# A two-layer graph network kernel: two of every 192 edge tiles fetched row by row from SyncE's queue

## What is computed

```python
h_s, h_v = s @ lin1_ws * a, v @ lin1_wv * a            # one row of 160 numbers for each node
w = silu(edge_scalars @ fc_w1) @ fc_w2                 # weights of each edge
es, ev = h_s[edge_src], h_v[edge_src]                  # gather: one row for each edge
m = ... w, es, ev, edge_attr ...                       # messages, 320 or 512 numbers an edge
agg = segment_sum(m, edge_dst)                         # add into the destination nodes
out = layernorm(x + node_update(agg, x))
```

## Time and profile before

| | us |
|---|---|
| median of 3 runs | 4140.89 |
| the runs | 4140.88, 4140.89, 4152.81 |
| the profiled execution | 4138.21 |
| span of its trace | 4136.5 |
| layer 0, first to last gather issued by POOL | 49.4 to 2003.3 |
| layer 1, first to last gather issued by POOL | 2099.9 to 4058.2 |

### The profile page before, as it was taken

How to read it: one execution, slowest core, us unless ns; L and a number is a source line. 1 busy time by engine, 2 the same in 40 slices (tenths; PEclk the granted TensorE clock), 3 DMA queues, 4 the chain that set the end, 5 groups by cost and what they waited for, 6 DMA issues and landing times. The chain is left out here.

```text
span 4136.5 us, 230757 instructions
## 1 busy us (share of the span) xinstructions
PE 3309.1 (80%) x91130; PEld 2547.6 (62%) x91131; DVE 2370.1 (57%) x6475; ACT 2897.3 (70%) x12105; POOL 3001.8 (73%) x3196
## 2 busy tenths in 40 slices
PE   8888888888777777777888888888878777777777
PEld 6666666666555555555766666666656565566556
DVE  6555555555444444444556666666666666666667
ACT  6666666666666666666477777777778777777776
POOL 5777777777777777777457777777777777777771
PEclk9999999999999999999999999999999999999998
DMA  5333333333222222222244334434333333333333
GB/s 156 83 84 84 83 83 83 83 86 83 73 73 73 72 73 73 73 73 72 83 123 108 104 105 109 106 104 108 105 105 98 94 94 96 94 94 96 94 94 111
DMA packets 361345, 381.19 MB, mean 92 GB/s; under 512 B 173457, under 2 KB 282677, under 8 KB 361182
## 3 DMA queue, kind: packets, MB, share of 16 engines
q0 software_dynamic: 150048, 256.28, 24.1%
q1 hardware_dynamic: 209936, 122.14, 10.4%
q10 hardware_dynamic: 1296, 1.91, 0.2%
HBM read 356.28 MB, written 23.76 MB: 92 GB/s over the span
## 5 line engine op out<-in xcount | busy, mean ns | idle before, releaser
L552 POOL DMA_INDIRECT e_rows<-scratch_table,k_index x3126 | 2954.9, 945 | 998.8 <-issue 886.1
L581 ACT ACTIVATE e_match<-e_match,e_attr 128x40 f32<-128x40 f32 x10976 | 2476.7, 316 | 0.0
L617 PE MATMUL e_sum<-e_match,e_msg 128*32 128x40 f32 (+1 forms) x81536 | 1440.6, 215 | 677.3 <-DVE e_msg L817 342.8
L617 PEld LDWEIGHTS e_sum<-e_match,e_msg 128*32 128x32 f32 x81536 | 1295.0, 111 | 995.8 <-DVE e_msg L820 376.4
L812 DVE TENSOR_TENSOR e_msg<-e_w,e_rows 128x512 f32<-128x512 f32 x784 | 541.9, 691 | 1656.4 <-DMA e_rows<-scratch_table,k_index 1608.5
L574 ACT ACTIVATE e_hidden<-e_h 100x512 f32<-100x512 f32 (+1 forms) x784 | 384.2, 490 | 1124.4 <-PE e_h L597 1116.6
L610 PE MATMUL e_w<-k_fc,e_hidden 100*128 100x192 f32 (+1 forms) x6272 | 1030.7, 367 | 0.8 <-issue 0.8
L610 PEld LDWEIGHTS e_w<-k_fc,e_hidden 100*128 100x128 f32 (+1 forms) x6272 | 812.3, 190 | 351.0 <-issue 333.0
L597 PE MATMUL e_h<-e_inputs,k_fc 128*100 128x512 f32 (+1 forms) x1568 | 713.3, 537 | 116.4 <-issue 63.7
L815 DVE TENSOR_TENSOR e_msg<-e_w,e_rows 128x384 f32<-128x384 f32 x784 | 428.7, 547 | 0.0
L817 DVE TENSOR_TENSOR e_msg<-e_w,e_rows 128x384 f32<-128x384 f32 x784 | 428.6, 547 | 0.0
(11 more groups left out here) (131 smaller groups left out, 1021.1 us busy)
## 6 DMA issues: line engine op xcount, KB each, us to landing
e_inputs<-in_inputs SPq DMA_DIRECT2D x196, 256.0 KB
e_rows<-scratch_table,k_index POOLq DMA_INDIRECT x3126
e_attr<-in_edge_attr SPq DMA_DIRECT2D x392, 24.0 KB
e_inputs<-in_inputs SPq DMA_DIRECT2D x196, 40.0 KB
e_xb<-in_xT SPq DMA_DIRECT2D x50, 128.0 KB
scratch_yT<-m_yT SPq DMA_DIRECT2D x10, 640.0 KB, 4.5
e_xb<-scratch_yT SPq DMA_DIRECT2D x50, 128.0 KB
k_index<-in_src SPq DMA_DIRECT2D x396, 4.0 KB, 3.2
```

The costliest lines, as they stand in the source:

```text
L552: pool.indirect_dma_start(out=rows[j][:, t, :], out_offset=None, in_=table_dram, in_offset=bass.IndirectOffsetOnAxis(ap=index[k][:, c:c + ...
L581: last = nc.scalar.activation(match[j][:, t, c, :], match[j][:, t, 4, :], ACT.Copy, scale=attr[q][:, e0 + t, e:e + 1])
L617: return nc.tensor.matmul(out[32 * g:32 * g + 32, c0:c0 + n, :], m[:, f:f + 32], m5[:, which:which + n, :], start=first and opens, stop=en ...
```

## The change

In each layer, after two bodies as before, the other 96 bodies run in 8 spans of 12. In bodies 5 and 11 of a span, counted from 0 (`FETCHED`), the last tile of group 1 is no longer gathered by POOL: POOL issues three gathers for that group (the last of them raises the semaphore by 32 in place of 16). That is 16 tiles a layer, 32 in all, so 3126 indirect DMAs become 3094.

These 32 tiles are fetched by SP. It reads their row numbers from a new small tensor, `row_index` (one 16x16 load for each span), eight numbers at a time into registers (`TENSOR_LOAD`), and issues one DMA for each row, 128 a tile, into `kept_rows[0]` or `kept_rows[1]`. A batch is one such load with its eight DMAs. `BATCHES` says how many batches stand behind the loads of q = 0 and q = 1 in each body of a span: (2, 1) in the first five bodies, 32 batches in twelve bodies in all. `attr[q]` is loaded in the middle of the first batch of its half. When a tile is complete, and group 1 of the body before is summed, SP issues one DMA that copies `kept_rows` to the fourth tile of `rows[1]` (`place_rows`).

A new semaphore, `placed`, goes up by 16 for each body: by the copy in the two bodies with a fetched tile, by an instruction of SP in the ten others, behind all their batches. DVE now also waits for it ahead of group 1's messages in every body, and SP waits for it once at the start of a span.

The loops become longer. In the built program POOL's branch goes back over 275 instructions (before 43), SP's over 841 and 793 (before 47 and 39). The loops of PE, DVE and ACT stay as they were; DVE's go back over 237 and 232 instructions, PE's over 317 and 314 in layer 0 and 436 in layer 1.

The core of the diff:

```diff
+FIRST, SPAN = 2, 12
+SPANS = (BODIES - FIRST) // SPAN
+BATCH = 8
+FETCHED, FETCHED_GROUP = (5, 11), 1
+BATCHES = ((2, 1),) * 5 + ((1, 1), (1, 1), (2, 1), (1, 1), (2, 1), (2, 1), (2, 0))
+PER_TILE = P // BATCH
...
+            def fetch_rows(batch, between=None):
+                which, batch = divmod(batch, PER_TILE)
+                _, numbers = nc.values_load_multi_w_load_instructions(
+                    row_index[batch:batch + 1, which * BATCH:which * BATCH + BATCH], engines=[sp.engine], min_val=0, max_val=NPAD - 1,
+                    skip_runtime_bounds_check_because="sources are node numbers")
+                for r in range(BATCH):
+                    if between and r == BATCH // 2:
+                        between()
+                    p = batch * BATCH + r
+                    sp.dma_start(kept_rows[which][p:p + 1, :], table_dram[bass.ds(numbers[r], 1), :]).then_inc(row_in[which], 16)
+
+            def place_rows(span, which):
+                landed, summed = 16 * P * (span + 1), GPB * (FIRST + SPAN * span + FETCHED[which] - 1) + FETCHED_GROUP + 1
...
+                sp.wait_ge(row_in[which], landed)
+                sp.wait_ge(sum_done, summed)
+                sp.dma_start(rows[FETCHED_GROUP][:, TPG - 1, :], kept_rows[which][:, :]).then_inc(placed, 16)
...
+            def fetching_body(span, position, with_base):
+                i, batch = FIRST + SPAN * span + position, sum(sum(b) for b in BATCHES[:position])
+                for q, batches in enumerate(BATCHES[position]):
+                    load_inputs(i, q, (2 * (position % 2) + q + 2) % INDEX_BUFFERS)
+                    if position == 0 and q == 0:
...
+                        sp.wait_ge(row_index_in, landed)
+                        sp.wait_ge(placed, free)
+                    if q == 1 and position in FETCHED:
+                        place_rows(span, FETCHED.index(position))
+                    for b in range(batches):
+                        fetch_rows(batch + b, (lambda: load_attr(i, q)) if b == 0 else None)
+                    batch += batches
+                    if not batches:
+                        load_attr(i, q)
+                if position not in FETCHED:
+                    sp.sem_inc(placed, 16)
+                if with_base:
+                    load_base(i)
+                if with_base and L == 1:
+                    store_self(i - 1)
+
+            def spans(first, last, with_base):
+                with sp.Fori(first, last) as span:
+                    for position in range(SPAN):
+                        fetching_body(span, position, with_base)
+                    load_row_index(span + 1)
...
+            spans(0, SPANS // 2, True)
             if L == 1:
                 store_self(NT - 1)
...
+            spans(SPANS // 2, SPANS, False)
...
+            def gather(i, position, j):
+                k = 2 * (position % 2) + j // 2
+                started = not isinstance(i, int)
+                if started:
+                    count, summed = 16 * (i - position % 2), GPB * i + j - GPB + 1
+                    pool.compute_val(count)
+                    pool.compute_val(summed)
...
+                fetched = started and position in FETCHED and j == FETCHED_GROUP
+                tiles = range(0 if started or i else EMPTY[j], TPG - 1 if fetched else TPG)
+                for t in tiles:
                     c = (j % 2) * TPG + t
...
-                    ).then_inc(gathered[j], 16)
...
+                    ).then_inc(gathered[j], 32 if fetched and t == tiles[-1] else 16)
...
+                if j == FETCHED_GROUP:
+                    dve.wait_ge(placed, 16 * i + 16)
```

More of the change, by code:

```diff
@@ L55, with fetched_tile @@
 GATHERED = 16 * TPG
+FIRST, SPAN = 2, 12
[4 more added lines that the diff above has]
+PER_TILE = P // BATCH
+assert FIRST + SPAN * SPANS == BODIES and (NT - FIRST) % SPAN == 0 and SPAN % 2 == 0
+assert sum(sum(b) for b in BATCHES[:6]) - 1 == PER_TILE and sum(sum(b) for b in BATCHES) == 2 * PER_TILE
+def fetched_tile(span, which):
+    return ((FIRST + span * SPAN + FETCHED[which]) * GPB + FETCHED_GROUP) * TPG + TPG - 1
 C_S, C_X = float(np.sin(np.pi / 8)), float(np.cos(np.pi / 8))
@@ L483, in _, with load_inputs @@
         def _(sp):
-            def load(i, q, k):
+            def load_inputs(i, q, k):
                 later = not (isinstance(i, int) and i == 0)
@@ L540, in _ @@
         def _(pool):
[L541 to L544, removed]
+            def gather(i, position, j):
[5 more added lines that the diff above has]
+                    pool.compute_val(summed)
                     pool.wait_ge(prepared, 1)
                     pool.wait_ge(index_in[k], count)
[L547 to L550, removed]
+                    pool.wait_ge(sum_done, summed)
+                elif i:
+                    pool.wait_ge(sum_done, GPB * i + j - GPB + 1)
+                fetched = started and position in FETCHED and j == FETCHED_GROUP
+                tiles = range(0 if started or i else EMPTY[j], TPG - 1 if fetched else TPG)
+                for t in tiles:
                     c = (j % 2) * TPG + t
@@ L554, in gather @@
                         in_offset=bass.IndirectOffsetOnAxis(ap=index[k][:, c:c + 1], axis=0),
[L555 to L556 removed]
+                    ).then_inc(gathered[j], 32 if fetched and t == tiles[-1] else 16)
+            for i in range(FIRST):
                 for j in range(GPB):
[L558 to L564 removed]
+                    gather(i, i, j)
+            with pool.Fori(0, SPANS) as span:
+                for position in range(SPAN):
                     for j in range(GPB):
[L566 removed]
+                        gather(FIRST + SPAN * span + position, position, j)
         @block.scalar
@@ L1241, in lay_out @@
     r["src"] = by_partition(padded(in_slots(a["src"]), EPAD + 2 * STEP * P))
+    by_tile = padded(in_slots(a["src"]), EPAD).reshape(T, PER_TILE, BATCH)
+    r["row_index"] = np.zeros((PER_TILE, SPANS + 1, 2, BATCH), np.int32)
+    for span in range(SPANS):
+        for which in range(2):
+            r["row_index"][:, span, which] = by_tile[fetched_tile(span, which)]
+    r["row_index"] = r["row_index"].reshape(PER_TILE, -1)
     dst = a["dst"][following]
```

42 lines of the change are left out of this document (25 added, 17 removed).

## The result

| | before | changed |
|---|---|---|
| median of 5 runs, us | 4140.88 | 4098.87 |
| the runs, us | 4139.96 to 4152.81 | 4098.42 to 4101.09 |
| span of the trace, us | 4136.5 | 4096.9 |

The changed kernel is faster: ratio 0.9895, 95% interval 0.9882 to 0.9909, which is 4097.4 us against the 4140.89 from which the forecast started. By span the difference is -39.6 us, by medians -42.0. The forecast was 4105, with a range from 4098.

What follows compares the result with a forecast made beforehand. POOL's own pace, one gather each 1.25 us, was taken to bound the kernel. -40.0 + 3 + 1 = -36 us gave 4102 against the profiled execution, and 2.7 us up to the median gave 4105; range 4098 to 4165.

Steps and rivals of the forecast that it cites:

- POOL's pace bounds; 32 gathers are worth 40.0 us: POOL in both edge phases: one gather each 1.25 us without other waits, so 32 fewer take off 40.0 us.
- The start of the layers: POOL waiting for sums where a layer starts: late inputs cost 0 to 2.2 us a layer, taken as 1 in all.
- Body 50: Layer 1, SP late at a store: 11.5 us of lateness against 8.5 that cost nothing, so 3 us once.
- The step to the median: From the profiled execution to the median of the runs: 2.7 us added, giving 4105.
- the range's low end: Lower edge of the forecast time: 4098, the full 40 us and 3 of scatter.
- SP's budget: SP's queue over twelve bodies: old loads, rows and register loads ask for 222 us of 237.5, so they fit.
- The lateness inside a span: SP's loads of q = 1 behind three batches' work come 2.2 us late, which costs nothing under 8.5 us.
- DVE's wait for `placed`: DVE ahead of group 1's messages: SP raises it at 19.2 us, wanted at 20.0, so it costs nothing.
- The range's upper end: Upper edge of the forecast time: 4165, said to belong to a register load of 1.75 us.
- The rival of SP as the bound: SP's queue: dearer register loads or rows make SP the bound; 4250 at 2.0 us a load, gain gone from 1.69; chance 0.21.
- The longer loop: POOL's branch back over 275 instructions, 14 times, costs time: 4113 to 4140; chance 0.10.
- the small DMAs: SP's row DMAs slow POOL's gathers; at 1% each, 39 us would go and 4144 remain; chance 0.03.

Runs made afterwards that it cites:

- e2: Changed kernel without SP's row-number loads, row DMAs and copies, POOL still leaving out its 32 gathers (stale rows summed): 4100.92 us, ratio 0.9907.
- e1: Changed kernel with SP's loads, rows and longer loops kept, but the copy left out and POOL gathering every tile: 4140.58 us against 4140.69, ratio 1.000.
- e9: The changed kernel itself, unaltered, run again in another set on one chip: 4103.05 us against 4142.22 for the kernel before, ratio 0.9907.
- e3: Changed kernel with each register load of eight row numbers made as four loads of two: 4207.22 us, ratio 1.0165.
- e15: POOL's 32 gathers left out and no rows fetched by SP, on a chip where PE stands: 6445.83 us, ratio 0.9951 to the kernel before.

## Where the prediction failed, and what in it held

**POOL's pace bounds; 32 gathers are worth 40.0 us: right.** Layer 0's part of the trace is 20.6 us shorter (the first gather of layer 1 is at 2078.95 for 2099.92, the first of all at 49.0 for 49.4), and e2 shows that the gathers alone do it.

**What failed is the end of the sum: the +3 and +1 us put back on POOL, and the 2.7 us from the profiled execution to the median.** The runs showed +0.2 in place of the +4, and nothing in place of the 2.7.

*The start of the layers, taken as +1: it was -0.9.* What POOL stood beyond its 0.30 us there was 1.78 us in layer 0 and 5.65 in layer 1 before, and is 0.52 and 6.03 now. e1 and e2, with the same loops, have 0.28 and 1.69 in layer 0, so this is scatter of one execution, not an effect of the change.

*Body 50, taken as +3: it is +1.1.* 0.28 us before, 0.45 + 0.90 now. The term was built as 8.8 us of old lateness and 2.7 of new row work against 8.5. e2 has pauses of 1.42 and 1.82 us there without any row work, 2.6 us beyond the usual 0.30, so the row work is not what they need; the 0.28 of one trace of before was a lucky reading of that place. In its second trace (e9) the changed kernel stands 1.49 and 1.86 us there, and the term would be +2.5.

*The step to the median, taken as +2.7.* The kernel before scatters from 4136.9 to 4152.8 on the usual chips, so 4138.2 for its profile and 4140.9 for its median are both draws from it; the changed kernel's profiled execution took 4098.87, exactly its median. That step added an offset where there was none to add.

Together: -40.0 - 0.9 + 1.1 = -39.8, and the spans differ by 39.6 where 36 was forecast. That is 3.6 us of the miss, the offset is 2.7, and both went the same way. Against the median of 4098.87 the forecast is 6 us off. The last 1.5 us come from the ratio, which compares means: that of the kernel before is 4142.95, because one of its five runs took 4152.81.

How small this is shows in e9: the same kernel in another set of runs took 4103.05 against 4142.22, a ratio of 0.9907. That would be 4102.4 on the forecast's scale, 2.6 us below it and inside the range. So the range's low end, 40 us and 3 of scatter, left too little room below the full gain, and scatter decided on which side of it the measurement fell; the interval of the first ratio, 4092 to 4103 us, reaches over that edge.

**SP's budget: right in its answer, wrong in its sizes, which cancel in part.** A row was taken at 0.54 us from two larger DMAs and takes 0.41; a load of eight was taken at 1.0 and takes 0.80. Old work was taken at 4.2 us a body, from the start of the first DMA to the end of the last, which leaves out the waits and addresses ahead of the first and the loop's branch. With them it is 5.0 in the kernel before and 5.3 now. 222 forecast, 201 found. The lateness inside a span was forecast at 2.2 us for q = 1 and is 0.3; DVE's wait for `placed` never mattered. The range's upper end has a slip of its own: by the same sum a load of 1.75 us gives 4157, and 4165 belongs to 1.78.

On the register load the Trainium skill, "Runtime: NRT & Kernel Launch", section on instruction fetch mechanics, gives about 200 ns a register, 1.6 us for eight: the trace disagrees, with 0.80. By its terms that page speaks of loads from HBM, and here the numbers lie in SBUF. The floor of 600 ns in the Trainium skill, "DMA: Bandwidth & Descriptors", section on latency and other measured facts, is undercut by the load of one number, 0.27 us in the median.

**The rival of SP as the bound (0.21)** had the right mechanism. Its price was off: at 2.32 us a batch it would have given 264 us for a first span, and e3 took 250. Going down from e3's 250 us to the 240 of the kernel before takes 0.31 us off each load, so the gain is gone at 2.0 us or a little above, where I had put 1.69. **The longer loop (0.10)** and **the small DMAs (0.03)** cost nothing that shows, by e1.

What I did not see at all is that the ground of the argument, POOL's pace as the bound, is a property of the chip at hand too. Where PE stands, the changed kernel with its last store moved takes 1.1% longer than the kernel before.

## What to carry to other kernels

Where one engine runs at its own pace without waiting, taking work off it is worth that work in full, and an idle queue can carry the replacement; sum what the queue is asked for over the whole period and over its worst stretch, and make the price of its unknown instruction dearer in one experiment, since that measures the spare room at once. Sum a queue's work from instruction to instruction: in the view of its DMAs alone one body looked like 4.2 us of work and was 5.0. And a term read from one execution needs the scatter of that place beside it, a pause of 0.28 us as much as a total.

## What the runs showed of the hardware

- A load of numbers from SBUF into SP's registers takes 0.27 us for one, 0.48 for two, 0.78 for eight and 1.22 for sixteen (medians; the next instruction starts some 0.04 later): less and less for each number.
- A DMA of one row of 640 bytes with an address from a register leaves SP every 0.41 us, and eight in a row still do (3.15 us for eight). 4096 of them did not lengthen an execution (4140.58 us against 4140.69).
- A gather of 128 rows of 640 bytes is busy for 945 ns in some executions and 948 in others, with SP's fetch (e1) and without it (e15).
- On three chips PE stood for 1.8 ms in all, mostly 0.5 or 1.2 us at a time, with nothing to wait for, and was busy for 1.2 ms more. With SP's fetch of 4096 rows it stood 112 us longer (1920.9 against 1809.3).
